# A decoder layer on one Trainium2 core: marks of all expert pairs counted at once in bf16, gates brought to their slots on chip

## Chip, cores and metric

One NeuronCore of a Trainium2 chip runs the whole layer in one launch. The time is device microseconds (us) of that core; lower is better. Values are f32 unless a tile is said to be bf16.

## What is computed

`x` (2048 tokens of 256) goes through causal self-attention on Plücker lines, cross-attention over 1601 context rows, and a mixture of 16 experts. The change lies in the last part:

```python
affinity = _sinkhorn(affinity_logits)          # 16 experts x 2048 tokens, 6 rounds
gates, idx = jax.lax.top_k(affinity, CAP)      # the 64 best tokens of each expert
expert_in = jnp.take_along_axis(x[:, None, :, :], idx[..., None], axis=2)
h = jax.nn.gelu(jnp.einsum('becd,edf->becf', expert_in, w1) + b1[None, :, None, :])
expert_out = jnp.einsum('becf,efd->becd', h, w2) + b2[None, :, None, :]
out = out.at[jnp.arange(b)[:, None, None], idx].add(gates[..., None] * expert_out)
```

## The kernel before

Everything up to the router is ordered by a planner; the change does not touch it. After it comes the tail, whose order on each engine is written by hand. It has three stages.

**Router.** VectorE does the Sinkhorn rounds, then finds the 64 best values of each of 8 chunks of tokens (`best_v`, `best_i`), and from them the limit of each expert (`limit`, L1590), counts over the chunks (`sums`), and the place at which each chunk's tokens go in its expert's list. It shifts each chunk's indices there in six doublings (L1619, L1620). TensorE turns and adds between these steps, and fills its waits with products that nobody reads: `keep_busy(n)` issues n of 128x256 (L1787). The engines run in order, so such products also hold back what stands behind them.

**Lists and pairs.** The product `tops` (L1957) adds the shifted lists up; VectorE casts them to `idx_gather` (L1629) and `idx_f`. Experts are taken in 8 pairs, 64 rows for each expert. GpSimd issues one indirect DMA for each pair's token rows (`gather_x`, L1090) and one for their affinities (L1098), from `affin_d`, which SyncE stored before. A token can be in both experts of a pair. So for each pair VectorE writes 128x256 of marks (`mark`, L1640 and L1641), TensorE adds them up over the partitions (`pair_sum`, L2008), and VectorE reads which rows repeat and which token numbers are free (`read_sums`, `place_rows`, L1648 to L1664). Two mark buffers are in turn.

**Experts.** For pair i: `expert_in(i)` turns the gathered rows (L1964), `hidden(i)` is the first product (L1977), `turn_hidden(i)` turns it (L1990), ScalarE does the gelu, `expert_out(i)` is the second product (L2001), `merge(i)` applies the gates and the merging of repeated rows (L2019), ScalarE copies the result (L1229), and GpSimd adds it to `out` by an indirect DMA (L1107), each behind the landing of the one before. SyncE loads the weights of experts 8 to 15 (L793, L798) and the bias rows (L966) as slots come free: the first of these wait for `hidden(0)` to be read on VectorE (`next_w1(0)`), and the others for later reads. Three PSUM banks (`g`) go round over the list `tail`: a step may write its bank only when VectorE has read the step three places before it.

## Time and profile before

| what | us |
|---|---|
| time of the runs shown, median (lowest, highest) | 1174.94 (1174.15, 1175.01) |
| profiled execution, its own time | 1175.17 |
| span of the profiled execution | 1173.4 |
| TensorE busy, VectorE busy, ScalarE busy, GpSimd busy in the span | 1105.5, 860.9, 718.2, 151.4 |

The span leaves out 1.8 us of the profiled execution's own time. Busy shares are averages over the whole program; the tail, from about 1030 us on, has other limits than the attention stages. The times in rows count from the start of the span.

### The profile page before, as it was taken

To read this page: it belongs to the slowest core of one execution; us is meant where nothing else is said; L and a number is where in the kernel's file an instruction comes from. 1 tells how busy PE (TensorE), PEld (TensorE's weight loads), DVE (VectorE), ACT (ScalarE), POOL (GpSimd) and SP (SyncE) were. 2 spreads that over 40 slices of the span, in tenths; PEclk is the share of its full clock that TensorE was granted. 3 is DMA by queue.
4 is the path that set the end of the run, shared out by engine and by line. 5 is a ranking of instruction groups with operands and counts; after the bars stand their busy time and mean duration, and the time that the engine had idled before them with its cause. 6 is when DMAs were issued, how large, how long until landed. Compare 5 with 4: busy or idle time off the path is not lost.

```text
span 1173.4 us, 30372 instructions
## 1 busy us (share of the span) xinstructions
PE 1105.5 (94%) x12600; PEld 525.7 (45%) x12600; DVE 860.9 (73%) x2017; ACT 718.2 (61%) x823; POOL 151.4 (13%) x260
## 2 busy tenths in 40 slices
PE   4788999999999999999999999999999999888997
PEld 2443433332432323544454456555555552467554
DVE  4888565487788878889788889788878980378631
ACT  0345567887678867677776877677785789310111
POOL 3024125112111011000001000010001000000522
PEclk9898999999999989999999999999999999998999
DMA  5113408722011000103232200111102000088696
GB/s 168 32 36 95 117 16 152 169 36 74 25 35 40 16 15 2 53 28 88 79 101 65 88 18 28 52 47 30 30 20 65 17 16 2 24 310 193 184 345 173
DMA packets 81562, 90.45 MB, mean 77 GB/s; under 512 B 18208, under 2 KB 73952, under 8 KB 81424
## 3 DMA queue, kind: packets, MB, share of 16 engines
q1 hardware_dynamic: 75264, 80.04, 23.9%
q10 hardware_dynamic: 4368, 6.29, 1.7%
q0 software_dynamic: 1792, 2.16, 1.0%
q8 instruction: 100, 1.64, 0.6%
q14 instruction: 38, 0.31, 0.1%
HBM read 73.42 MB, written 15.04 MB: 75 GB/s over the span
## 4 chain that ended last, share of the span: by engine, by line
PE 76%; DVE 11%; DMA 5%; issue 4%; ACT 2%; POOL 1%; ACTq 0%; DVEq 0%; POOLq 0%
PE po L1778 24%; PE g L1886 16%; PE scores L1754 15%; PE scores L1758 6%; PE g L1871 3%; PE g L1831 2%; ACT probs L1194 2%; DMA out<-self_region,idx_scatter 1%; DVE mx L1465 1%; PE g L1821 1%; PE g L1861 1%; DMA out<-wo_sb,idx_scatter 1%; PE scores L1787 1%; DMA out<-wxq_sb,idx_scatter 1%; PE g L1977 1%
## 5 line engine op out<-in xcount | busy, mean ns | idle before, releaser
L1194 ACT ACTIVATE probs<-scores 128x1024 f32<-128x1024 f32 (+2 forms) x736 | 677.0, 968 | 239.7 <-PE scores L1754 131.3
L1465 DVE TENSOR_REDUCE mx<-g 128x1 f32<-128x400 f32 (+1 forms) x1024 | 526.4, 567 | 86.2 <-PE g L1886 76.6
L1886 PE MATMUL g<-cross_region,even_region 96*32 96x400 bf16 (+1 forms) x4096 | 310.5, 338 | 0.4
L1754 PE MATMUL scores<-even_region,cross_region 99*32 99x512 bf16 (+1 forms) x3264 | 255.0, 379 | 2.5 <-ACT probs L1194 2.5
L1778 PE MATMUL po<-probs,cross_region 128*32 128x512 f32 (+1 forms) x1664 | 225.3, 594 | 0.8 <-ACT probs L1194 0.8
L1886 PEld LDWEIGHTS g<-cross_region,even_region 96*32 96x32 bf16 x4096 | 123.3, 95 | 182.9 <-DVE mx L1465 81.9
L1778 PE MATMUL po<-probs,self_region 128*32 128x512 f32 (+3 forms) x1280 | 152.1, 550 | 4.5 <-POOL probs L1055 3.9
L1754 PEld LDWEIGHTS scores<-even_region,cross_region 99*32 99x32 bf16 (+1 forms) x3264 | 100.9, 96 | 96.0 <-issue 42.6
L1758 PE MATMUL scores<-self_region 36*128 36x512 bf16 (+3 forms) x640 | 104.9, 360 | 7.2 <-ACT probs L1194 6.8
L1055 POOL TENSOR_SCALAR_AFFINE_SELECT probs<-probs 128x256 f32<-128x256 f32 x128 | 58.8, 468 | 276.7 <-ACT probs L1194 275.9
L1022 POOL TENSOR_TENSOR rstd<-mv,half 128x1 f32<-128x1 f32 x48 | 26.7, 556 | 518.5 <-DVE mv L1273 518.3
L1758 PEld LDWEIGHTS scores<-self_region 36*128 36x128 bf16 x640 | 26.6, 94 | 126.1 <-ACT probs L1194 76.9
L1778 PEld LDWEIGHTS po<-probs,cross_region 128*32 128x32 f32 (+1 forms) x1664 | 56.8, 110 | 24.9 <-ACT probs L1194 6.4
L1224 ACT ACTIVATE even_region<-scores 128x1024 f32<-128x1024 f32 x4 | 4.1, 1026 | 85.8 <-PE scores L1990 85.8
L1787 PE MATMUL scores<-xbo_sb,ident 128*128 128x256 f32 x190 | 51.4, 424 | 0.0
L1778 PEld LDWEIGHTS po<-probs,self_region 128*32 128x32 f32 x1280 | 30.9, 110 | 33.6 <-POOL probs L1055 13.5
L1821 PE MATMUL g<-ident,xn 128*128 128x128 f32 x96 | 21.0, 305 | 25.7 <-DVE xn L1327 25.6
L1787 PEld LDWEIGHTS scores<-xbo_sb,ident 128*128 128x128 f32 x190 | 39.5, 214 | 6.3 <-issue 0.2
L1439 DVE RECIPROCAL rsum<-g 128x16 f32<-128x16 f32 x32 | 8.2, 255 | 45.7 <-PE g L1861 45.5
L1831 PE MATMUL g<-wself_sb,xn_t 128*128 128x512 f32 x64 | 34.3, 662 | 0.1
L1450 DVE TENSOR_TENSOR xb<-g,xb 128x256 f32<-128x256 f32 x32 | 13.6, 424 | 28.1 <-PE g L1871 27.3
L1821 PEld LDWEIGHTS g<-ident,xn 128*128 128x128 f32 x96 | 10.4, 146 | 42.9 <-issue 31.0
(287 smaller groups left out, 881.3 us busy)
## 6 DMA issues: line engine op xcount, KB each, us to landing
cross_region<-in_w SPq DMA_DIRECT2D x16, 1024.0 KB, 12.8
even_region<-xq_d SPq DMA_DIRECT2D x192, 64.0 KB, 2.3
self_region<-in_w ACTq DMA_DIRECT2D x6, 1024.0 KB, 6.6
self_region<-in_w SPq DMA_DIRECT2D x6, 1024.0 KB, 13.8
cross_region<-xk_d SPq DMA_DIRECT2D x24, 200.1 KB, 8.0
xb<-in_x SPq DMA_DIRECT2D x32, 128.0 KB, 2.8
xb<-x_d SPq DMA_DIRECT2D x32, 128.0 KB, 2.4
probs<-in_w SPq DMA_DIRECT2D x4, 1024.0 KB, 13.2
```

The lines of the kernel that those rows point to most:

```text
L1022: pool.tensor_tensor(rstd[:, u % 4:u % 4 + 1], mv[:, u % 4, 1:2], half[:, 0:1], ALU.pow).then_inc(rstd_ready, 1)
L1055: pool.affine_select(out=d, in_=d, compare_op=ALU.is_ge, fill=0.0, base=0, pattern=[[0, 2], [1, P]], channel_multiplier=-1).then_inc(mask_ ...
L1194: act.activation(probs[0:rows, s % 4, :, off:], ps[s % 2][0:rows, :, off:], ACT.Exp, scale=LSCALE if QUADS[n][0] == "self" else 1.0).then_ ...
L1465: dve.reduce_max(mx[:, k % 2, b, h, c:c + 1], g[:, 0:n_keys], AX_X).then_inc(g_free, 1)
L1754: mm = pe.matmul(ps[s % 2][c:c + n_keys, a, :], k_cross[0:NS * DH + 3, h, i * P + c:i * P + c + n_keys], rhs, start=True, stop=True)
L1758: mm = pe.matmul(ps[s % 2][0:rows, a, off:], lhs, rhs, start=True, stop=True)
L1778: mm = pe.matmul(po[32 * a:32 * a + 32, off:], v[0:rows, i, h * VW:h * VW + 32], probs[0:rows, s % 4, a % 2, off:], start=(i == 0), stop=e ...
L1787: pe.matmul(ps[0][:, 0, 0:D], ident[:, :], xbo_sb[:, :], start=True, stop=True)
L1821: mm = pe.transpose(g[:, k * P:(k + 1) * P], xn[:, norm_no[u] % 2, k * P:(k + 1) * P], ident[:, :])
L1831: pe.matmul(g[:, :], xn_t[:, k, c + 1:c + 1 + P], wself_sb[:, k, 0:512], start=(k == 0), stop=False)
L1871: mm = pe.matmul(g[:, 0:D], attn_t[:, k, :], (wo_sb if step[1] == "self" else wxo_sb)[:, k, :], start=(k == 0), stop=(k == DK - 1))
L1886: mm = pe.matmul(g[q:q + 32, 0:n_keys], q_max[k % 2][0:NS * DH, h, b * P + q:b * P + q + 32], k_cross[0:NS * DH, 4 * (k % 4) + h, start:st ...
```

## The change

The marks of all eight pairs are written by one VectorE instruction of 128x1024 in bf16 (`mark_tokens`) and counted by two bf16 products, before the first gathered rows are turned. Which rows repeat is read from eight small products (128x64) of the lists themselves, which follow `tops`. The gates are no longer stored and gathered: VectorE shifts the values `best_v` as it shifted the indices, in `shifted_v`, and one more product (`gates`) adds them up to their slots. Of the unread products, 15 become 18 ahead of `best_t`, and 12 become 17 ahead of `tops`; two after `tops` become one and two, written to `po`. Lines that are only "..." stand for what is left out.

```diff
-    affin_d = nc.dram_tensor("affin_d", (T, E), F32, kind="Internal").ap()
...
-        kept = o_region[:, 1344:1344 + CAP]
+        kept = late_region[:, 264:264 + CAP]
...
-        bits = o_region[:, 1436:1442]
-        others = o_region[:, 1442:1448]
+        bits = late_region[:, 328:334]
+        others = late_region[:, 334:340]
...
-        picked_affin = late_region[:, 256:256 + E // 2 * E].rearrange("p (i e) -> p i e", e=E)
+        gates = late_region[:, 256:256 + E // 2]
+        shifted_v = [even_region[:, 1024 + 2 * CAP * r:1024 + 2 * CAP * (r + 1)] for r in range(2)]
...
-        marks = [attn[:, :], attn_t[:, :, :].rearrange("p k n -> p (k n)")]
+        marks = o_region[:, 1536:2048].bitcast(BF16).rearrange("p (i n) -> p i n", i=E // 2)
+        ones_b = attn[:, 0:P // 2].bitcast(BF16)
...
-        affin_stored = sem("affin_stored")
-        gates_gathered = [sem(f"gates_gathered{i}") for i in range(E // 2)]
+        values_ready = sem("values_ready")
...
         tail = ["col_turn", "col_back"] + [("col_sum", it) for it in range(SINK_ITERS)]
...
-                 ("h", 1, 0), ("h", 1, 1)]
+                 ("h", 1, 0), ("h", 1, 1), "gates"]
         for i in range(E // 2):
...
-            sp.wait_ge(router_pe, 3 + SINK_ITERS)
-            sp.dma_start(affin_d.rearrange("(b p) e -> p b e", p=P), affin[:, :, :]).then_inc(affin_stored, 16)
...
+            pool.wait_ge(g_full, NG)
+            pool.memset(attn[:, 0:P // 2], BF16_ONES).then_inc(const_ready, 1)
...
             pool.wait_ge(picked, 2)
-            pool.wait_ge(affin_stored, 16)
...
             for i in range(E // 2):
...
                     gather_x(i + 2)
-                pool.indirect_dma_start(
-                    picked_affin[:, i, :], None, affin_d, bass.IndirectOffsetOnAxis(idx_gather[:, i:i + 1], 0)
-                ).then_inc(gates_gathered[i], 16)
...
             for i in range(E // 2):
...
+            def move(bufs, k):
+                src, dst = bufs[k % 2], bufs[1 - k % 2]
+                link(dve.tensor_scalar(kept, src[:, CAP:2 * CAP], others[:, k:k + 1], None, ALU.mult))
+                return dve.scalar_tensor_tensor(out=dst[:, CAP:2 * CAP],
+                                                in0=src[:, CAP - (1 << k):2 * CAP - (1 << k)],
+                                                scalar=bits[:, k:k + 1], in1=kept, op0=ALU.mult, op1=ALU.add)
...
-                src, dst = shifted[k % 2], shifted[1 - k % 2]
-                link(dve.tensor_scalar(kept, src[:, CAP:2 * CAP], others[:, k:k + 1], None, ALU.mult))
-                last = dve.scalar_tensor_tensor(out=dst[:, CAP:2 * CAP], in0=src[:, CAP - (1 << k):2 * CAP - (1 << k)],
-                                                scalar=bits[:, k:k + 1], in1=kept, op0=ALU.mult, op1=ALU.add)
+                last = move(shifted, k)
...
-            def mark(i):
-                if i >= 2:
-                    dve.wait_ge(pair_sums, i - 1)
-                link(dve.tensor_scalar(marks[i % 2][:, 0:P], ident[:, :], idx_f[:, i:i + 1], None, ALU.mult))
-                dve.tensor_scalar(marks[i % 2][:, P:2 * P], row_no, idx_f[:, i:i + 1], None,
-                                  ALU.is_equal).then_inc(marked, 1)
-            def read_sums(q):
-                four = slice(4 * q, 4 * q + 4)
-                dve.wait_ge(pair_sums, 4 * q + 4)
-                sums = ps[q][:, :, :].rearrange("p a b -> p (a b)").rearrange("p (i n) -> p i n", i=4)
-                link(dve.tensor_tensor(mix[:, four, 0:CAP], sums[:, :, 0:CAP],
-                                       idx_f[:, four].unsqueeze(2).broadcast_to((P, 4, CAP)), ALU.is_equal))
-                dve.scalar_tensor_tensor(out=unused[:, four, :], in0=sums[:, :, P:2 * P], scalar=0.0,
-                                         in1=row_no.unsqueeze(1).broadcast_to((P, 4, P)), op0=ALU.is_equal,
+            def mark_tokens():
+                dve.tensor_tensor(marks, row_no.unsqueeze(1).broadcast_to((P, E // 2, P)),
+                                  idx_f.unsqueeze(2).broadcast_to((P, E // 2, P)), ALU.is_equal).then_inc(marked, 1)
+            def read_sums():
+                dve.wait_ge(pair_sums, 2)
+                link(dve.tensor_tensor(mix[:, :, 0:CAP], ps[0][:, 0, :].rearrange("p (i n) -> p i n", n=CAP),
+                                       idx_f.unsqueeze(2).broadcast_to((P, E // 2, CAP)), ALU.is_equal))
+                counts_of = ps[1][:, :, :].rearrange("p a b -> p (a b)").rearrange("p (i n) -> p i n", n=P)
+                dve.scalar_tensor_tensor(out=unused, in0=counts_of, scalar=0.0,
+                                         in1=row_no.unsqueeze(1).broadcast_to((P, E // 2, P)), op0=ALU.is_equal,
                                          op1=ALU.mult).then_inc(sums_read, 1)
...
             def place_rows():
-                dve.wait_ge(sums_read, 2)
+                dve.wait_ge(sums_read, 1)
...
-                dve.wait_ge(gates_gathered[i], 16)
-                for e in range(2):
-                    rows = slice(CAP * e, CAP * (e + 1))
-                    last = dve.tensor_scalar(mix[rows, i, :], mix[rows, i, :],
-                                             picked_affin[rows, i, 2 * i + e:2 * i + e + 1], None, ALU.mult)
-                last.then_inc(mixed, 1)
+                dve.tensor_scalar(mix[:, i, :], mix[:, i, :], gates[:, i:i + 1], None, ALU.mult).then_inc(mixed, 1)
...
-            for i in range(4):
-                mark(i)
+            mark_tokens()
+            for r in range(2):
+                link(dve.memset(shifted_v[r][:, 0:CAP], 0.0))
+            link(dve.scalar_tensor_tensor(out=shifted_v[0][:, CAP:2 * CAP], in0=row_no[:, 0:CAP], scalar=n_here,
+                                          in1=best_v, op0=ALU.is_lt, op1=ALU.mult))
+            link(move(shifted_v, 0))
+            link(move(shifted_v, 1))
             expert_in(0)
             expert_in(1)
-            mark(4)
-            mark(5)
-            read_sums(0)
+            link(move(shifted_v, 2))
+            read_sums()
             hidden(0)
-            mark(6)
-            mark(7)
             expert_in(2)
-            read_sums(1)
+            for k in range(3, 5):
+                link(move(shifted_v, k))
+            move(shifted_v, 5).then_inc(values_ready, 1)
             hidden(1)
+            g = tail_full(dve, "gates")
+            for e in range(2):
+                last = dve.tensor_copy(gates[CAP * e:CAP * (e + 1), :],
+                                       g[0:CAP, 0:E].rearrange("p (i e) -> p e i", e=2)[:, e, :])
+                if e == 0:
+                    link(last)
+            last.then_inc(g_free, 1)
+            dve.wait_ge(g_free, TF["gates"])
             place_rows()
             for i in range(E // 2):
...
-            def keep_busy(n):
+            def keep_busy(n, bank=ps[0][:, 0, 0:D]):
...
-                    pe.matmul(ps[0][:, 0, 0:D], ident[:, :], xbo_sb[:, :], start=True, stop=True)
+                    pe.matmul(bank, ident[:, :], xbo_sb[:, :], start=True, stop=True)
...
-            keep_busy(15)
+            keep_busy(18)
             g = tail_bank(pe, "best_t")
...
-            keep_busy(12)
+            keep_busy(17)
             g = tail_bank(pe, "tops")
...
             pe.matmul(g[0:CAP, 0:E], shifted[0][:, CAP:2 * CAP], same_expert[:, 0:E], start=True, stop=True).then_inc(g_full, 1)
+            pe.wait_ge(exp_done, 2 * len(QUADS))
+            for i in range(E // 2):
+                mm = pe.matmul(ps[0][:, 0, CAP * i:CAP * (i + 1)], same_expert[:, 2 * i:2 * i + 1].broadcast_to((P, P)),
+                               shifted[0][:, CAP:2 * CAP], start=True, stop=True)
+            mm.then_inc(pair_sums, 1)
...
-                    pe.wait_ge(sums_read, i + 1)
+                    pe.wait_ge(sums_read, 1)
...
-            def pair_sum(i):
-                pe.wait_ge(marked, i + 1)
-                pe.matmul(ps[i // 4][:, i % 4 // 2, i % 2 * 2 * P:(i % 2 + 1) * 2 * P], ones[:, :], marks[i % 2],
-                          start=True, stop=True).then_inc(pair_sums, 1)
+            def count_marks():
+                pe.wait_ge(const_ready, 17)
+                pe.wait_ge(marked, 1)
+                for half_of in range(2):
+                    mm = pe.matmul(ps[1][:, half_of, :], ones_b, marks[:, 4 * half_of:4 * half_of + 4, :],
+                                   start=True, stop=True)
+                mm.then_inc(pair_sums, 1)
...
-            keep_busy(2)
-            pe.wait_ge(exp_done, 2 * len(QUADS))
-            for i in range(4):
-                pair_sum(i)
+            pe.wait_ge(o_free, len(evacs))
+            keep_busy(1, po[:, 0:D])
+            count_marks()
+            keep_busy(2, po[:, 0:D])
             expert_in(0)
             expert_in(1)
             hidden(0)
-            pair_sum(4)
-            pair_sum(5)
             expert_in(2)
-            pair_sum(6)
-            pair_sum(7)
             hidden(1)
+            g = tail_bank(pe, "gates")
+            pe.wait_ge(values_ready, 1)
+            pe.matmul(g[0:CAP, 0:E], shifted_v[0][:, CAP:2 * CAP], same_expert[:, 0:E], start=True, stop=True).then_inc(g_full, 1)
             turn_hidden(0)
             for i in range(E // 2):
...
```

How the instructions move. TensorE from the product `tops` to the first hidden product: before, with the pair sums as L2008,

```order
L1787 MATMUL scores<-xbo_sb,ident 128x256 x12
L1957 MATMUL g<-bo_sb,o_region 64x16
L1787 MATMUL scores<-xbo_sb,ident 128x256 x2
L2008 MATMUL scores<-attn,late_region 128x256
L2008 MATMUL scores<-attn_t,late_region 128x256
L2008 MATMUL scores<-attn,late_region 128x256
L2008 MATMUL scores<-attn_t,late_region 128x256
L1964 MATMUL g<-ident,self_region 128x128 x4
L1977 MATMUL g<-self_region 64x512 x8
```

and in the changed kernel, where L1962 is `tops`, L1966 the list products, L2021 the count and L1988 the hidden product:

```order
L1792 MATMUL scores<-xbo_sb,ident 128x256 x17
L1962 MATMUL g<-bo_sb,o_region 64x16
L1966 MATMUL scores<-o_region,bo_sb 128x64 x8
L1792 MATMUL po<-xbo_sb,ident 128x256
L2021 MATMUL scores<-o_region,attn 128x512 x2
L1792 MATMUL po<-xbo_sb,ident 128x256 x2
L1975 MATMUL g<-ident,self_region 128x128 x4
L1988 MATMUL g<-self_region 64x512 x8
```

The four pair sums ahead of the first transposes are gone; eight list products, two counts and one more unread product stand there. TensorE between `hidden(0)` and `hidden(1)`, before:

```order
L2008 MATMUL scores<-attn,late_region 128x256
L2008 MATMUL scores<-attn_t,late_region 128x256
L1964 MATMUL g<-ident,wo_sb 128x128 x2
L2008 MATMUL scores<-attn,late_region 128x256
L2008 MATMUL scores<-attn_t,late_region 128x256
L1977 MATMUL g<-self_region 64x512
```

and in the changed kernel, with the end of `hidden(1)` and the product of the gates (L2046) behind it:

```order
L1975 MATMUL g<-ident,wo_sb 128x128 x2
L1988 MATMUL g<-self_region 64x512
...
L1988 MATMUL g<-cross_region,self_region 64x512
L2046 MATMUL g<-bo_sb,even_region 64x16
L2001 MATMUL scores<-ident,even_region 128x128 x8
```

Four pair sums have left this place and one small product has come behind `hidden(1)`. VectorE in the changed kernel, from the marks (L1639) to the reading of `hidden(0)` (L1674); L1610 and L1611 are one doubling of the values, L1665 the copies of turned rows, L1644 and L1647 the reading of the sums:

```order
L1639 TENSOR_TENSOR o_region<-bv_sb 128x1024
L1690 MEMSET even_region 128x64 x2
L1691 SCALAR_TENSOR_TENSOR even_region<-bv_sb,o_region 128x64
...
L1665 COPY self_region<-g 128x256 x2
L1610 TENSOR_SCALAR late_region<-even_region,late_region 128x64
L1611 SCALAR_TENSOR_TENSOR even_region<-even_region,late_region 128x64
L1644 TENSOR_TENSOR o_region<-scores,bv_sb 128x8x64
L1647 SCALAR_TENSOR_TENSOR o_region<-scores,bv_sb 128x1024
L1674 TENSOR_TENSOR even_region<-g,even_region 128x512 x2
```

Before, eight pairs of L1640 and L1641 and two readings of half the size stood between L1630 and `hidden(1)`.

## Rows read from the trace of the kernel before

**Rows 1.** Window: PE, PEld, DVE, ACT, POOL busy us, clock, DMA share, GB/s.

```profile
1110.00:1120.00 10.00, 10.00 (x75) 5.48 (x70) 2.70 (x6) 1.29 (x2) 1.62 (x1) 1.00 1.04 285
```

**Rows 2.** Chain that ended last: start us, us, what.

```profile
1114.71 9.84 DMA out<-self_region,idx_scatter
...
1158.15 3.79 DMA out<-wxq_sb,idx_scatter
...
1167.26 1.55 POOL out L1107
```

**Rows 3.** Timeline of ScalarE: the last copy.

```profile
1166.06 0.37 ACT L1229 COPY wxo_sb<-po 128x256 f32<-128x256 f32 x1 [4.48 <-PE po L2019]
```

**Rows 4.** Timeline of TensorE, limit stage; each f32 product counts as two matmuls.

```profile
1056.40 6.64 PE L1787 MATMUL scores<-xbo_sb,ident 128*128 128x256 f32 x30
1064.59 0.27 PE L1930 MATMUL g<-ident,o_region 128*64 128x128 f32 x1 [1.55 <-DVE o_region L1562]
...
1066.91 9.48 PE L1787 MATMUL scores<-xbo_sb,ident 128*128 128x256 f32 x30
1076.31 0.38 PE L1947 MATMUL g<-o_region,bo_sb 16*128 16x8 f32 x2
...
1078.45 5.43 PE L1787 MATMUL scores<-xbo_sb,ident 128*128 128x256 f32 x24
1086.42 0.37 PE L1957 MATMUL g<-bo_sb,o_region 128*64 128x16 f32 x2 [2.54 <-DVE o_region L1620]
```

**Rows 5.** Windows of 2 us: the clock after each of two waits.

```profile
1066.00:1068.00 2.00, 2.00 (x11) 1.62 (x12) 1.49 (x6) 0.00 (x0) 0.00 (x0) 0.50 1.02 229
1086.00:1088.00 2.00, 1.57 (x5) 1.39 (x6) 1.28 (x7) 0.00 (x0) 0.52 (x1) 0.53 0.00 0
```

**Rows 6.** Timeline of VectorE around the limit.

```profile
1075.16 0.42 DVE L1567 FIND_INDEX8 o_region<-o_region,even_region 128x8 uint32<-128x256 f32 x1
1076.80 0.17 DVE L1590 COPY o_region<-g 128x8 f32<-128x8 f32 x1 [1.22 <-PE g L1947]
```

**Rows 7.** Timeline of GpSimd, first gathers; landing time of the second.

```profile
1087.48 1.21 POOL L1090 DMA_INDIRECT self_region<-xn_d,idx_gather  x1 [52.58 <-DVE idx_gather L1629]
1089.00 0.96 POOL L1090 DMA_INDIRECT self_region<-xn_d,idx_gather  x1 [0.31 <-issue]
...
DMA to landing us min/median/max: 2.8/2.8/2.8
```

**Rows 8.** Timeline of TensorE, first transposes to the last second product.

```profile
1091.44 0.89 PE L1964 MATMUL g<-ident,self_region 128*128 128x128 f32 x4
1092.54 3.65 PE L1977 MATMUL g<-self_region 128*64 128x512 f32 x16 [0.21 <-DVE self_region L1668]
...
1098.71 0.64 PE L1977 MATMUL g<-self_region 128*64 128x512 f32 x1
...
1107.89 3.62 PE L2001 MATMUL g<-self_region,even_region 128*64 128x256 f32 x32
...
1161.10 0.43 PE L2001 MATMUL g<-cross_region,self_region 128*64 128x256 f32 x1
```

**Rows 9.** Timelines and chain: rows nearest to the new instructions.

```profile
1078.02 0.35 PE L1952 MATMUL g<-o_region,bo_sb 128*128 128x2 f32 x2 [0.26 <-DVE o_region L1594]
1078.23 0.36 PE L1953 MATMUL g<-o_region,bo_sb 128*128 128x2 f32 x2
...
1082.94 0.30 DVE o_region L1620
...
1103.73 1.22 DVE L1657 TENSOR_REDUCE bv_sb<-o_region 128x8 f32<-128x1024 f32 x1
```

**Rows 10.** Queue of SyncE: first and last of the late loads.

```profile
1096.95 0.50 SPq L966 DMA_DIRECT2D even_region<-in_b  x1
...
1147.27 3.40 SPq L798 DMA_DIRECT2D probs<-in_w  x1
...
probs<-in_w SPq DMA_DIRECT2D x1, 1024.0 KB, 12.6
```

## Prediction

> **What bounds the kernel now.** I read the chain that ended last from its end backwards. Its last part is the eight indirect DMAs that add the expert rows to `out`, from 1114.71 on. Each waits for the landing of the one before: 9.84 us for the first, 3.79 for the sixth, and the last is issued at 1167.26 [rows 2]. Read alone, this says that the additions are the bound. The timeline of ScalarE corrects it: the last copy, which the last addition needs, begins at 1166.06 and takes 0.37 [rows 3]. So it is done at 1166.43, 0.83 before the last issue. Two chains arrive together, the additions and TensorE's expert products, and TensorE has no free time in the expert stage (10.00 of 10 us busy, clock 1.00, DMA share 1.04 [rows 1]). An edit pays only if it starts both chains sooner, so the question is when `expert_out(0)` starts; before, that is 1107.89 [rows 8]. The end also depends on the late weight loads, which fill the DMA engines [rows 1].
>
> **Unread products.** The 15 ahead of `best_t` end at 1063.04 (1056.40 + 6.64), and `best_t` comes at 1064.59 after 1.55 us of idle time. The clock is then 0.50 in the window of 1066 to 1068 [rows 4, 5], its lower level of 1.2 GHz. The 15 products ahead of `limit` take 9.48 us where the first 15 took 6.64, 2.8 us more [rows 4]. VectorE has ended its own searches at 1075.58 and gets the limit only at 1076.80 [rows 6]. A product costs 0.443 us at the full clock (6.64 / 15), so 18 end at 1064.4, just ahead of 1064.59: they delay nothing and leave 0.2 us idle instead of 1.55. I take it that the clock then stays at 2.4 GHz. The products ahead of `limit` end near 1073.6, TensorE is no longer the later one, and VectorE goes on at 1075.6: **1.2 us**. Lower end nothing (the clock falls all the same); upper end 1.2, since VectorE's searches bound it.
>
> The 17 ahead of `tops`: 12 take 5.43 us, 0.453 each, so 17 take 7.7. From 1078.45 they end at 1086.15, against `tops` at 1086.42 [rows 4]. Both shift together, so they are hidden by VectorE's shifting, with 0.27 us to spare at the full clock. Without that cover each costs 0.45 or, at half the clock, 0.9.
>
> **From the lists to `hidden(0)`.** The gathers follow the lists as before. The second is issued at 1089.00, lands 2.8 later, at 1091.8 [rows 7], and `hidden(0)` begins at 1092.54 [rows 8]. In between stand both transposes and a copy, because the pair sums held the first transpose until the second gather had landed. In the changed kernel TensorE has, behind `tops`, eight list products, a count in two, and three unread products. The list products are nearest to L1952 and L1953, which start 0.21 apart [rows 9]: 8 x 0.21 = 1.7 us (upper end 3.5, the price of unread products, 8 x 0.443). The three unread products are 1.35, the counts at most as much as a 128x256 f32 product each, 0.9. In all 3.6 to 4.0 us behind `tops` (1086.42 + 0.37 = 1086.8), so 1090.4 to 1090.8: about when the first gather lands (1087.48 + 3.0), and ahead of the second. The first transpose and its copy are then over before 1091.8, and `hidden(0)` follows the second transpose by some 0.3: 1092.2, **0.35 us** sooner. Lower end: list products at 3.5 push this to 1092.6 or so, no gain; upper end 0.5.
>
> VectorE's marks: 128x1024 lies nearest to the reduce of 128x1024, 1.22 us [rows 9]; below it can't be under half of that. They are needed when the list products are over, 1.7 us after `tops`, and it has them about 0.3 us later than that, which the one unread product ahead of the count covers.
>
> **Between `hidden(0)` and `expert_out(0)`.** From 1096.19 (1092.54 + 3.65) to 1098.71 TensorE does four pair sums and one pair of transposes [rows 8]. Only the transposes stay, 0.22: **2.3 us**. Behind `hidden(1)` comes the product of the gates, **-0.2** [rows 9]. Could VectorE now be late? After the second copy it has one doubling of the values (0.6), the reading of both sums (0.7 and 1.2, by the row of 128x1024), then `hidden(0)`'s first half (0.7): 3.2 us behind a copy that ends 0.6 after `hidden(0)` begins. That is 3.8, where TensorE needs the bank back after 3.65 + 0.22. It is nearly a tie; I take off **0.1**, and the lower end is 1 us. Behind the reading of `hidden(1)` stand the gate copies and the eight instructions of `place_rows`, the longest of them 1.22 us [rows 9]; I put both together at 4.2, and the copy of `xe` 3 behind them at 0.4. They begin near 1099.5 in the changed kernel and end near 1104.1, and `expert_out(0)` wants the bank of `xe` 3 at 1104.3. That is a second near tie: nothing is taken off, and each 0.1 us by which VectorE is later there comes off the gain. The gathers and the copy of the affinities that go take GpSimd time which lies beside other work.
>
> Sum for TensorE: 1.2 + 0.35 + 2.3 - 0.2 - 0.1 = 3.55 us sooner at `expert_out(0)`. All later steps of TensorE, and the first addition, shift with it.
>
> **What comes late next.** The late loads start when `hidden(0)` is read (1096.95 [rows 10]). That trigger comes only 1.2 + 0.3 = 1.5 us sooner, because the saving of 2.3 lies behind it, and from there the DMA engines are full. Six token gathers no longer stretch into that time, perhaps 0.6 us of transfer, and the second trigger comes 3.6 sooner into engines that are not quite full: together the loads end 2 to 2.5 us sooner. Before, the last one is issued at 1147.27 and lands after 12.6, 1159.9 [rows 10]; `expert_out(7)` wants it at 1161.10 [rows 8], a slack of 1.2. Then it lands at 1157.6 and is wanted at 1157.55: the slack is gone. The additions meet the same: the sixth was quick, 3.79, since the loads were ending; issued 3.5 sooner it has 3 us of loads before it. I take off **0.7** for both (bounds 0 and 2.0, the case where the loads keep their time but for 1.5).
>
> 3.55 - 0.7 = 2.85. Against the profiled execution's own 1175.17 that is 1172.3. The median of the runs shown is 0.2 under that execution, which may be in the clock's part of the tail; so I say 1172.2.
>
> **A rule against the change.** The first gathers are issued while VectorE works on the marks and doublings; in the rows the first takes 1.21 on GpSimd and the second 0.96, with VectorE busy there too [rows 7]. The Trainium skill, SBUF — State Buffer, section on the doors (the "DVE blocks DMA" trap), says that a DMA issued by GpSimd can't get its descriptors written while VectorE runs an instruction that takes both ports. By the rows, the most that such a wait can have cost a gather is 0.25 us (1.21 - 0.96). This is a rival with 3 in 100: both first gathers later by 0.25 each, the time 1172.7. By that rule it would come through the memsets and multiplications, which are in both kernels.
>
> **Rivals.**
> Forecast as above, 50 in 100: 1171.3 to 1173.0.
> The clock falls ahead of `limit` all the same, 22 in 100. For it: the short products of `best_t` and the candidates keep TensorE half idle after the long ones, and 1.55 us of idle time sufficed before. The 1.2 us is lost: 1173.4.
> The late loads set the end, 18 in 100. For it: DMA share 1.04 [rows 1]. If only the first trigger's 1.5 us come through, 1175.17 - 1.5 = 1173.7.
> Slower, 7 in 100: the longer rows of unread products become the path. If the clock is at its lower level when the 17 begin and stays there, they take 17 x 0.886 = 15.1 us where VectorE's chain leaves 8.0 (1078.45 to 1086.42 [rows 4]). The other gains are 3.55 - 1.2 = 2.35, so the 17 make the kernel slower from a length of 10.3 us on; at full length they give 1175.2 + 7.1 - 2.35 = 1179.9.
> The additions alone being slowed by as much as they start sooner is the upper part of the third case, up to 1174.
>
> **How the numbers follow.** 0.2% of this time is 2.35 us, which is about what a measurement can tell; it lies at 1172.6, close to the forecast. Faster by more: most of the forecast's 50 and a little of the others, 52. Slower by more: most of the slow case and nothing else, 5. Within: 43. The range reaches over the two cases at 1173.4 and 1173.7 with their uncertainty of 0.3: 1170.9 to 1174.0. The lower end is the sum with no loss to the loads, 1175.17 - 3.55 = 1171.6, less the 0.2 of the median, and 0.5 for additions that find the engines freer.
>
> **What would show it.** Right: granted clock 1.00 in 1066 to 1076, the copy of the limit 1.2 us sooner; `hidden(0)` at about 1091.0, `hidden(1)` at 1094.9, `expert_out(0)` at 1104.3; the last load landing near 1157.6; the last addition issued near 1164.4. Wrong: clock 0.5 before `limit`; VectorE's L1647 ending after TensorE wants the bank; idle time of TensorE on a load ahead of `expert_out(7)`; additions that land later after their issue than before; unread products that end after their list is ready.

## The result and the profile after

The changed kernel takes 1168.05 us (median of 5 runs, 1167.61 to 1169.26), the kernel before 1174.39 (5 runs, 1172.11 to 1175.01). The ratio is 0.9953 with a 95% interval of [0.9939, 0.9966]: 4.0 to 7.2 us faster, where 2.2 were forecast (1174.39 - 1172.2). Measured again on two chips, it was 0.9951 (e5) and 0.9953 (e16). The time lies 2.9 us below the lower end of the range, 1170.9. The profiled execution has a span of 1166.3 us (before 1173.4).

**A place to start from.** The two profiled spans differ by 7.1 us, but not all of it is the edit. TensorE's first short transpose behind the 15 (now 18) unread products stands at 1064.59 before [rows 4] and at 1061.49 after, 3.1 us sooner, and ahead of it the edit only adds three products that fill a wait. The windows far ahead of the edit show where most of such differences come from; the columns are as in [rows 1]. First before:

```profile
420.00:430.00 10.00, 8.51 (x69) 2.26 (x68) 5.65 (x16) 6.37 (x8) 0.00 (x0) 0.70 0.16 42
430.00:440.00 10.00, 10.00 (x102) 2.78 (x98) 7.04 (x14) 6.72 (x8) 0.00 (x0) 0.79 0.00 0
```

and the same stretch of the changed kernel:

```profile
420.00:430.00 10.00, 8.51 (x108) 2.91 (x104) 7.88 (x21) 7.86 (x9) 0.32 (x1) 1.00 0.14 42
430.00:440.00 10.00, 10.00 (x122) 2.97 (x116) 8.05 (x16) 8.21 (x9) 0.00 (x0) 1.00 0.01 2
```

TensorE is busy for 8.51 us of the first window in both, but gets through 69 products in one and 108 in the other: the granted clock was 0.70 and 0.79 in one execution and 1.00 in the other. By ScalarE's timelines, where both kernels have the same instructions up to here, before is 1.35 us ahead at 409.32 (410.67 after) and 3.24 us behind at 438.89 (435.65 after), so the fall costs about 4.6 us. Of the 16 later profiles four have a clock of 0.61 to 0.71 in the first of these windows (e2, e3, e8, e11), with and without parts of the edit. So I count from that transpose to the end: 108.8 us before (1173.4 - 1064.59), 104.8 after (1166.3 - 1061.49), **4.0 us shorter**.

TensorE's timeline of the changed kernel from there, to be held against [rows 4] and [rows 8]:

```profile
1061.49 0.27 PE L1935 MATMUL g<-ident,o_region 128*64 128x128 f32 x1 [0.25 <-DVE o_region L1558]
1063.41 6.74 PE L1792 MATMUL scores<-xbo_sb,ident 128*128 128x256 f32 x30
1071.34 0.35 PE L1952 MATMUL g<-o_region,bo_sb 16*128 16x8 f32 x2 [1.19 <-DVE o_region L1582]
...
1073.37 0.35 PE L1957 MATMUL g<-o_region,bo_sb 128*128 128x2 f32 x2 [0.61 <-DVE o_region L1590]
...
1073.81 9.27 PE L1792 MATMUL scores<-xbo_sb,ident 128*128 128x256 f32 x34
1083.01 0.29 PE L1962 MATMUL g<-bo_sb,o_region 128*64 128x16 f32 x2
1083.23 2.00 PE L1966 MATMUL scores<-o_region,bo_sb 128*128 128x64 f32 x16
...
1088.72 3.65 PE L1988 MATMUL g<-self_region 128*64 128x512 f32 x16
...
1101.92 3.62 PE L2012 MATMUL g<-self_region,even_region 128*64 128x256 f32 x32
```

The wait ahead of `best_t` is 0.25 us instead of 1.55, and the 15 products ahead of `limit` take 6.74 instead of 9.48. TensorE now waits for VectorE at `limit` (1.19), not the other way round. Then, new: the 17 ahead of `tops` take 9.27 us, and the timeline of VectorE shows who pays:

```profile
1072.16 0.17 DVE L1586 COPY o_region<-g 128x8 f32<-128x8 f32 x1
...
1083.34 0.35 DVE L1630 CAST idx_gather<-g 64x8 uint32<-64x8 f32 x2 [1.69 <-PE g L1962]
...
1090.49 1.23 DVE L1647 SCALAR_TENSOR_TENSOR o_region<-scores,bv_sb 128x1024 f32<-128x1024 f32 x1
1091.63 1.48 DVE L1674 TENSOR_TENSOR even_region<-g,even_region 128x512 f32<-128x512 f32 x2
```

It waits 1.69 us for `tops`. The 2-us windows give the reason, a low clock behind the limit, which no profile of another kernel here has at this place:

```profile
1066.00:1068.00 2.00, 2.00 (x11) 1.77 (x10) 1.86 (x7) 0.00 (x0) 0.00 (x0) 1.00 1.02 234
1074.00:1076.00 2.00, 2.00 (x6) 1.62 (x6) 1.79 (x9) 0.00 (x0) 0.00 (x0) 0.55 0.04 8
1076.00:1078.00 2.00, 2.00 (x7) 1.59 (x7) 1.67 (x10) 0.00 (x0) 0.00 (x0) 0.60 0.00 0
```

So the 4.0 us come about as: transpose to limit copy 12.21 to 10.67 (1.54 gained), limit copy to `tops` 9.62 to 10.85 (1.23 lost), `tops` to `hidden(0)` 6.12 to 5.71 (0.41), `hidden(0)` to `expert_out(0)` 15.35 to 13.20 (2.15), from there to the last copy of ScalarE 58.17 in both. The rest, 1.13 us, is at the very end, and the prediction does not have it. ScalarE's last copy and GpSimd's additions:

```profile
1160.09 0.37 ACT L1225 COPY wxo_sb<-po 128x256 f32<-128x256 f32 x1 [4.47 <-PE po L2033]
```

```profile
1118.69 1.56 POOL L1103 DMA_INDIRECT out<-self_region,idx_scatter  x1 [8.33 <-DMA out<-self_region,idx_scatter]
...
1134.31 1.55 POOL L1103 DMA_INDIRECT out<-wo_sb,idx_scatter  x1 [6.21 <-ACT wo_sb L1225]
...
1160.73 1.55 POOL L1103 DMA_INDIRECT out<-wxo_sb,idx_scatter  x1 [3.16 <-ACT wxo_sb L1225]
```

Only the second and third addition still wait for the landing of the one before; from the fourth on each waits for ScalarE's copy. The last is issued 0.64 us behind the start of the last copy, before 1.20 [rows 2, 3]: 0.56 less in this pair of profiles. And the span ends 5.57 us behind that issue instead of 6.14 (1173.4 - 1167.26): 0.57 more. The late loads, on SyncE's queue:

```profile
1093.14 1.13 SPq L966 DMA_DIRECT2D even_region<-in_b  x2
...
1097.09 1.12 SPq L966 DMA_DIRECT2D even_region<-in_b  x2
...
1139.04 3.36 SPq L798 DMA_DIRECT2D probs<-in_w  x1
...
probs<-in_w SPq DMA_DIRECT2D x1, 1024.0 KB, 12.7
```

The last one is issued 8.2 us sooner than before (1147.27 [rows 10]), or 5.1 sooner when counted from the transpose. It lands near 1151.7 (1139.04 + 12.7), 3.5 us ahead of `expert_out(7)`, which begins at 1155.20 by the chain that ended last (in e5 and e16 it lands 2.2 and 2.3 us ahead):

```profile
1155.20 3.60 PE g L2012 x32
```

### The profile page after: what moved, and what is told of

Same layout as the page of the kernel before. It is cut to its first block, busy times and chain, and to the rows that moved or that the text cites. A ratio compares the mean times of both kernels' runs of the same rounds, so it can differ in the third digit from the quotient of the medians.

```text
span 1166.3 us, 30403 instructions
## 1 busy us (share of the span) xinstructions
PE 1101.0 (94%) x12622; PEld 525.5 (45%) x12622; DVE 859.5 (74%) x2009; ACT 718.2 (62%) x823; POOL 145.6 (12%) x253
## 4 chain that ended last, share of the span: by engine, by line
PE 82%; DVE 10%; issue 3%; ACT 2%; POOL 1%; DMA 1%; ACTq 0%; DVEq 0%
PE po L1783 24%; PE g L1891 16%; PE scores L1759 15%; PE scores L1763 6%; PE g L1876 3%; PE g L1836 3%; PE g L1988 2%; PE g L2012 2%; ACT probs L1190 2%; PE g L1826 1%; PE g L1866 1%; PE scores L1792 1%; DVE mx L1461 1%; PE g L1882 1%; PE g L1870 1%
## 5 line engine op out<-in xcount | busy, mean ns | idle before, releaser
L1763 PE MATMUL scores<-self_region 36*128 36x512 bf16 (+3 forms) x640 | 103.5, 356 | 7.5 <-ACT probs L1190 7.2
```

The costliest lines, as they stand in the source:

```text
L1763: mm = pe.matmul(ps[s % 2][0:rows, a, off:], lhs, rhs, start=True, stop=True)
```

## Experiments

The kernels e1 to e4 ran on one chip, e5 to e8, e9 to e12 and e13 to e16 each on another. The kernel before took 1181.7, 1172.95, 1172.24 and 1173.36 us there (medians of 17 to 35 runs).

**e1, the unread products alone, in the kernel before.**

```diff
-            keep_busy(15)        # ahead of best_t
+            keep_busy(18)
-            keep_busy(12)        # ahead of tops
+            keep_busy(17)
```

> The kernel before with only the numbers of unread products changed (15 to 18 ahead of best_t, 12 to 17 ahead of tops). Theory A (the 18 keep the clock at its full level ahead of limit): granted clock 1.00 between the candidates and limit, the copy of the limit 1.2 us sooner against the stage's start, and the whole kernel 1 to 1.5 us under the kernel before. Rival B (the large surplus over the forecast comes from the products too): 3 us or more under it. Rival C (the surplus comes from a fall of the clock at 424 us, which is no part of the edit): this kernel's own profile may or may not have that fall, and its time goes with it by about 4.6 us.

Measured 1181.8 us, ratio 0.9999 [0.9987, 1.0011]. The clock was 1.00 from 1064 to 1080 and the limit copy came 10.65 us behind the transpose, yet no gain shows on this chip; the interval leaves room for 1.5 us. `hidden(0)` to `expert_out(0)` took 27.1 us. The chain of e1 in that stretch:

```profile
1094.22 3.29 another core or an unknown queue
...
1098.69 7.31 another core or an unknown queue
```

TensorE's and ScalarE's timelines, same kernel:

```profile
1098.16 1.09 PE L1990 MATMUL scores<-ident,even_region 128*128 128x128 f32 x8
1107.43 1.97 PE L1990 MATMUL scores<-ident,self_region 128*128 128x128 f32 x8 [8.18 <-DVE self_region L1677]
```

```profile
1106.20 1.02 ACT L1224 ACTIVATE even_region<-scores 128x1024 f32<-128x1024 f32 x1 [69.04 <-remote]
```

ScalarE's gelu needs only TensorE's transposes, which end at 1099.25; it starts at 1106.20. VectorE stands still from 1098.7 to 1106.1 as well. What both wait for is no instruction in the trace.

**e2, the changed kernel with the old numbers.**

```diff
-            keep_busy(18)
+            keep_busy(15)
-            keep_busy(17)
+            keep_busy(12)
```

> The changed kernel with the old numbers of unread products (15 ahead of best_t, 12 ahead of tops). Theory A: 1.2 us over the changed kernel by the limit stage, and up to 1 us more where a clock at 1.2 GHz behind tops holds back the list products; 1.2 to 2.2 us in all, the tail being 71.5 us or so in place of 69.9 from the first router instruction. Rival B (the products do more than that): 3 us or more over it. Rival (they do nothing): the same as the changed kernel.

Measured 1171.68 us, ratio 0.9914 [0.9895, 0.9932]: 10 us faster than before on that chip. `hidden(0)` to `expert_out(0)` is 13.2 us; the long wait of e1 is not there. `hidden(0)` follows `tops` by 7.91 us, where the changed kernel has 5.67 to 5.71: e12 returns to this.

**e3, the changed kernel with the affinities stored and gathered as before.** No doublings of values, no gates product; the marks and the products are the changed kernel's.

```diff
+                pool.indirect_dma_start(picked_affin[:, i, :], None, affin_d,
+                    bass.IndirectOffsetOnAxis(idx_gather[:, i:i + 1], 0)).then_inc(gates_gathered[i], 16)
-            pe.matmul(g[0:CAP, 0:E], shifted_v[0][:, CAP:2 * CAP], same_expert[:, 0:E], ...)
```

> The changed kernel with the gates stored and gathered as before, so without the doublings of the values and the product of the gates. Theory: the gates' part is worth nothing or a little less than nothing on TensorE (one product of 0.1 to 0.2 us is gone from the path), so the time is within 0.4 us of the changed kernel. Rival: the eight gathers of affinities slow GpSimd's token gathers and the late loads, and their removal was worth 0.5 us or more, so this one is slower by that.

Measured 1179.34, ratio 0.9978 [0.9967, 0.9989], with the long wait (21.5 us from `hidden(0)` to `expert_out(0)`).

**e4, the kernel before with two unread products in the wait near 421 us.**

```diff
+                    if step[1] == 3:
+                        for _ in range(2):
+                            pe.matmul(g[:, 0:D], ident[:, :], xbo_sb[:, :], start=True, stop=True)
                     pe.wait_ge(shift_split, step[1] + 1)
```

> The kernel before with two unread products of 128x256 in the PSUM bank of the fourth shift_turn, where TensorE waits 0.7 and 0.8 us near 421 us. Theory C (in most runs of the kernel before, the clock falls there for some 10 us and costs 4.6 us, whatever stands in the tail): granted clock 1.00 from 420 to 440, and 3 to 4.6 us under the kernel before in the median. Rival D (the whole surplus lies in the tail): within 0.5 us of the kernel before.

Measured 1182.17, ratio 1.0000 [0.9988, 1.0011]. Its profile has no low clock there, but neither has that of e1, which lacks the two products. Filling this wait changes nothing that the times show, on a chip where the long wait (24.2 us from `hidden(0)` to `expert_out(0)` in e4) hides much.

These four gave a new theory: gathering the affinities, which the prediction priced at nothing, costs time. The next four tested it, on a chip where no profile shows the long wait.

**e5, the changed kernel again.**

> The changed kernel itself, on the chip of the next three runs. If the chip has the long wait between hidden(0) and expert_out(0) in kernels that gather the affinities (27.1 us in e1 where the first chip's profile of before had 15.35), the changed kernel has 13.2 there and ends 10 to 13 us below before, of which the unread products (18 and 17 for 15 and 12) give at most 2: e2 had 1171.7 with the old numbers. Rival (no such wait, the gain is what the prediction summed): 3 to 6 us below before.

Measured 1167.61, ratio 0.9951 [0.9935, 0.9968]. The rival held: no long wait on this chip. This profile has the clock at 1.00 from 1064 on, and from the transpose to the end it is 103.5 us, 5.3 shorter than before. Its `tops` is on time:

```profile
1074.28 7.58 PE L1792 MATMUL scores<-xbo_sb,ident 128*128 128x256 f32 x34
1082.25 0.26 PE L1962 MATMUL g<-bo_sb,o_region 128*64 128x16 f32 x2 [0.39 <-DVE o_region L1611]
1082.44 2.00 PE L1966 MATMUL scores<-o_region,bo_sb 128*128 128x64 f32 x16
...
1087.92 3.65 PE L1988 MATMUL g<-self_region 128*64 128x512 f32 x16
```

**e6, the kernel before without the store and the gathers of the affinities.** The rows are weighted with a constant, so the gates are left out.

```diff
-            sp.dma_start(affin_d.rearrange("(b p) e -> p b e", p=P), affin[:, :, :]).then_inc(affin_stored, 16)
-                pool.indirect_dma_start(picked_affin[:, i, :], None, affin_d, ...)
-                                             picked_affin[rows, i, 2 * i + e:2 * i + e + 1], None, ALU.mult)
+                                             first_half[rows, 0:1], None, ALU.mult)
```

> Before without the store and the eight gathers of the affinities; the rows are weighted with a constant, so the gates are left out. Marks, pair sums and unread products are those of before. Theory (the small gathers hold TensorE's signals back between hidden(0) and expert_out(0)): 6 to 9 us below before, hidden(0) to expert_out(0) 15 to 16 us. Rival (the pair sums between the products cost the time, the gathers lie beside other work, as the prediction had it): within 0.5 us of before.

Measured 1170.72, ratio 0.9987 [0.9977, 0.9996]: 1.5 us by the ratio, 2.2 by the medians, between the two expectations. `hidden(0)` to `expert_out(0)` is 15.32, as before. SyncE's queue, with the second trigger of the late loads at 1099.76 and the last load:

```profile
1099.76 1.12 SPq L966 DMA_DIRECT2D even_region<-in_b  x2
...
1108.64 9.01 SPq L798 DMA_DIRECT2D self_region<-in_w  x2
...
1139.69 3.20 SPq L798 DMA_DIRECT2D probs<-in_w  x1
```

Its transpose stands at 1062.49, so the last load is issued 77.20 us behind it. That is as soon as in the changed kernel (77.55 to 78.38), although the order is the old one.

**e7, the changed kernel with the store and eight gathers that nobody reads.** GpSimd waits for them ahead of its first addition.

```diff
+            sp.dma_start(affin_d.rearrange("(b p) e -> p b e", p=P), affin[:, :, :]).then_inc(affin_stored, 16)
                     gather_x(i + 2)
+                pool.indirect_dma_start(picked_affin[:, i, :], None, affin_d, ...).then_inc(gates_gathered[i], 16)
             pool.wait_ge(placed, 1)
+            for r in range(E // 2):
+                pool.wait_ge(gates_gathered[r], 16)
```

> The changed kernel with the store and the eight gathers of the affinities put back at their old places, into columns that nobody reads; only GpSimd waits for them, at the row additions. Theory (the small gathers hold TensorE's signals back): 6 to 9 us above the changed kernel, with a wait of VectorE for hidden(1) of more than 4 us. Rival (they lie beside other work): within 0.5 us of the changed kernel.

Measured 1171.14, ratio 0.9987 [0.9973, 1.0001], 3.5 us above e5 by the medians. VectorE has no long wait; the theory's mechanism is not there, but the cost is. GpSimd's timeline shows it:

```profile
1111.70 1.62 POOL L1116 DMA_INDIRECT out<-self_region,idx_scatter  x1 [8.01 <-DMA late_region<-affin_d,idx_gather]
...
1154.40 1.55 POOL L1116 DMA_INDIRECT out<-wxq_sb,idx_scatter  x1 [6.55 <-DMA out<-wxq_sb,idx_scatter]
```

The last gather, issued at 1102.75, had not landed before 1111, and the additions were late from there to the end. The waits of TensorE show a second cost, a late load that it stood still for:

```profile
PE g L2025 <- DMA probs<-in_w: 1.2, 1, 1.2
```

**e8, the kernel before with the affinity gathers behind all token gathers.**

```diff
                 if i + 2 < E // 2:
                     gather_x(i + 2)
+            for i in range(E // 2):
                 pool.indirect_dma_start(picked_affin[:, i, :], None, affin_d, ...)
```

> Before with the eight affinity gathers behind all eight token gathers instead of between them. Theory A (any of the sixteen gathers that is under way with the late loads holds the signals back): same as before within 1 us. Theory B (what matters is a token gather that comes late because an affinity gather stands ahead of it): 5 to 9 us below before. Rival (gathers are hidden): within 0.5 us of before, and no long wait in either.

Measured 1172.56, ratio 0.9998 [0.9987, 1.0008]. Their place in the order is worth nothing that the interval shows (1.5 us at most).

**e9, as e7, but GpSimd waits for the idle gathers only at the end.**

```diff
-            for r in range(E // 2):
-                pool.wait_ge(gates_gathered[r], 16)
...
             pool.wait_ge(scattered, 16 * (E // 2))
+            for i in range(E // 2):
+                pool.wait_ge(gates_gathered[i], 16)
```

> As e7, but GpSimd waits for the eight idle affinity gathers only behind the last row addition; in e7 it waited ahead of the first, which began 3.75 us later than in the changed kernel. Theory (in e7 that wait cost the time, the gathers only load the DMA engines a little): ratio to before 0.995 to 0.997, that is 0 to 2 us above the changed kernel, the first addition about 6.9 us behind expert_out(0). Rival (the gathers themselves delay the late loads or the additions): ratio 0.998 to 0.999, the additions still the last chain.

Measured 1168.77, ratio 0.9978 [0.9965, 0.9990]. The median fits the theory (its wait was e7's largest cost), the ratio lies between both. In its profile every stage is as in e5, and only the end differs: 6.27 us from the last issue, not 5.57. So this profile shows 0.7 of the 3 us between the ratios.

**e10, e3 on this chip.**

> The changed kernel with the affinities stored and gathered again and read by expert_out, as e3, on another chip. Without the long wait of e1 and e3 between hidden(0) and expert_out(0), that stretch is 13.0 us (13.2 less the gates product), and the time is 0 to 2 us above the changed kernel: ratio to before 0.995 to 0.997. Rival: the affinity gathers cost 3 to 4 us in this form too, 0.998 to 0.999.

Measured 1169.42, ratio 0.9985 [0.9970, 0.9999], with 13.13 us from `hidden(0)` to `expert_out(0)`. By the median it is in the theory's range, by the ratio in the rival's. From the transpose to the end its profile has 104.2 us, 0.7 more than e5.

**e11, e1 on this chip.**

> Before with 18 and 17 unread products, as e1, on another chip. Prediction's term: 1.2 us for the clock, 1.55 by the profiles since; as before's runs have the low clock ahead of limit in most but not all cases, 0.8 to 1.5 us below before, ratio 0.9987 to 0.9993. Rival: the 17 cost as much as the 18 give (the first profile of the changed kernel had tops 1.2 us late), ratio 0.9995 to 1.0005.

Measured 1171.25, ratio 0.9994 [0.9982, 1.0006], 1.0 us below before by the medians, with an interval that holds zero. The profile says more. TensorE's timeline:

```profile
1084.20 0.26 PE L1957 MATMUL g<-bo_sb,o_region 128*64 128x16 f32 x2 [0.40 <-DVE o_region L1620]
...
1089.57 0.41 PE L1964 MATMUL g<-ident,self_region 128*128 128x128 f32 x2 [0.61 <-DMA self_region<-xn_d,idx_gather]
1089.91 3.65 PE L1977 MATMUL g<-self_region 128*64 128x512 f32 x16
```

With 17 products the clock is 1.00 behind `tops`, the pair sums are over before the second gather has landed, and `hidden(0)` follows `tops` by 5.71 us: as in the changed kernel, with all four pair sums still in their old place. GpSimd's last addition and SyncE's queue in the same kernel:

```profile
1164.20 1.55 POOL L1107 DMA_INDIRECT out<-wxo_sb,idx_scatter  x1 [3.10 <-ACT wxo_sb L1229]
```

```profile
1109.51 11.33 SPq L798 DMA_DIRECT2D self_region<-in_w  x2
...
1144.31 3.42 SPq L798 DMA_DIRECT2D probs<-in_w  x1
```

**e12, the changed kernel with 12 instead of 17 products ahead of `tops`, 18 ahead of `best_t`.**

```diff
-            keep_busy(17)
+            keep_busy(12)
```

> The changed kernel with 12 unread products ahead of tops, 18 ahead of best_t as it has. If the 17 only fill a wait, within 0.5 us of the changed kernel (ratio 0.9948 to 0.9957), or above it where the clock falls behind tops; if they are late in a share of the runs, up to 1 us below it (ratio 0.9940 to 0.9948).

Measured 1170.54, ratio 0.9988 [0.9974, 1.0001]: 2.9 us above e5, which ran on another chip, by the medians, and 4.3 by the ratios. It is the case that the expectation names beside its numbers, the clock that falls behind `tops`. TensorE's timeline of e12, against e5's above, tells why:

```profile
1082.75 0.26 PE L1962 MATMUL g<-bo_sb,o_region 128*64 128x16 f32 x2 [2.56 <-DVE o_region L1611]
1082.94 3.34 PE L1966 MATMUL scores<-o_region,bo_sb 128*128 128x64 f32 x16
...
1089.60 0.88 PE L1975 MATMUL g<-ident,self_region 128*128 128x128 f32 x4
1091.02 3.65 PE L1988 MATMUL g<-self_region 128*64 128x512 f32 x16 [0.54 <-DVE self_region L1665]
```

and its windows (TensorE's busy time, clock, DMA):

```profile
1084.00:1086.00 2.00, 2.00 (x11) 0.50 0.17 41
```

The list comes at the same time, but behind 2.56 us of idle time the clock is at its lower level. List products, counts, unread products and transposes all take longer, and `hidden(0)` follows `tops` by 8.27 us instead of 5.67: 2.6 us.

**e13, as e9, with one semaphore for the eight idle gathers instead of eight.**

```diff
-                ).then_inc(gates_gathered[i], 16)
+                ).then_inc(gates_gathered, 16)
```

> As e9 (the changed kernel with eight idle affinity gathers, waited for at the end), but all eight count on one semaphore instead of one each. From the issue of the last addition to the end of the span e9 has 6.27 us, the changed kernel 5.57. If the seven further semaphores that are used cost that time: 5.6 to 5.7. If the gathers or their store cost it: 6.2 to 6.3.

Measured 1170.21, ratio 0.9977 [0.9968, 0.9986]. The end took 6.33 us (last addition issued at 1162.07, span 1168.4). So the number of semaphores is not the cause of the 0.6. TensorE also waited 0.7 for the last load here, which was issued at 1144.20:

```profile
PE g L2024 <- DMA probs<-in_w: 0.7, 1, 0.7
```

**e14, the changed kernel with more products around the limit**, as an attempt to end the low clock of the first profile.

```diff
-            keep_busy(15)        # ahead of limit
+            keep_busy(17)
-            keep_busy(2)         # ahead of sums
+            keep_busy(3)
```

> The changed kernel with 17 instead of 15 unread products ahead of limit and 3 instead of 2 ahead of sums: TensorE's idle 1.19 and 0.61 us there become 0.3 and 0.2. If the clock falls there in a share of the runs, as in the first profile of the changed kernel (0.5 from 1074.1, tops 1.2 us late): median 0.2 to 1.0 us below e16, and fewer times at the upper end. Rival (that fall is rare, or the products are late themselves): within 0.3 us of e16.

Measured 1168.59, ratio 0.9962 [0.9947, 0.9976], above e16's 1167.80 by 0.8. Neither profile has the low clock there, and from the transpose to the end both have 103.7 us. The attempt shows no gain; whether it would end that fall is not tested.

**e15, the changed kernel with 15 instead of 18 products ahead of `best_t`.**

```diff
-            keep_busy(18)
+            keep_busy(15)
```

> The changed kernel with 15 instead of 18 unread products ahead of best_t. By the prediction's term the low clock ahead of limit comes back where it falls: limit 1.55 us later in such runs, the median 0.5 to 1.6 us above e16. Rival (only the 17 matter): within 0.3 us of e16.

Measured 1168.87, ratio 0.9964 [0.9950, 0.9979], 1.1 us above e16 by the medians. That is not shown to be the clock's doing: the intervals overlap, and e15's profile, whose own time of 1168.92 is its median, has no low clock ahead of the limit (10.66 us from the transpose to the limit copy, 103.9 to the end, against 103.7 in e16).

**e16, the changed kernel a third time.**

> The changed kernel again, as the measure for e13, e14 and e15 on their chip: ratio to before 0.9945 to 0.996; router to limit 43.8 us, limit to tops 9.62, tops to hidden(0) 5.7, hidden(0) to expert_out(0) 13.2, 5.57 from the last addition's issue to the end. On a chip with the long wait of e1 in before: ratio 0.989 to 0.991.

Measured 1167.80, ratio 0.9953 [0.9938, 0.9969].

## Why the prediction was wrong, by its steps

The direction was right, and two of the three gains on TensorE came for the reason given. The size was short by 2.4 us: 2.85 forecast; from the transpose on 5.3 in e5 and 5.1 in e16, against the profile of before.

**Clock ahead of the limit, forecast 1.2: right, larger.** 1.54 in the first profile. The upper end of 1.2 took VectorE's searches as the bound, but they are filled in between the rounds and shift with it: the limit copy comes right behind a search, without a wait. It is a gain of some executions only. With 15 products the transpose to the limit copy takes 12.21 us in the profiles of before and e8, 11.03 in e4 (clock 0.50 in 1062 to 1064) and 10.66 in e2, e6 and e15; with 18 it takes 10.65 to 10.67 in all twelve profiles. The rival in which the clock falls ahead of the limit all the same did not come. By the medians the 18 (e15) and the 18 and 17 together (e11) give about 1 us, which the intervals don't separate from nothing.

**The 17 ahead of `tops`, priced at nothing: wrong.** I looked only at what they cost and cited the cover that hides them. The time from `tops` to `hidden(0)` in the profiles shows what they give:

| from `tops` to `hidden(0)`, us | 12 products | 17 products |
|---|---|---|
| old order (pair sums first) | 6.12 (before), 6.11 (e8), 6.42 (e6), 7.15 (e4) | 5.67 (e1), 5.71 (e11) |
| new order (list products first) | 7.91 (e2), 8.27 (e12) | 5.66 to 5.72 (all) |

With 17 the two orders take the same. With 12 the clock falls behind `tops` in all six profiles, and that costs 0.4 to 1.5 us in the old order and 2.2 to 2.6 in the new one, where eight list products stand there at once. In the other direction, the first profile of the changed kernel has the clock at 0.55 while the 17 run, and `tops` 1.23 us late. That is the slower rival's mechanism at a small size. One of the three profiles of the changed kernel has it (e5 and e16 do not). How often it comes in the timed runs is not known.

**`hidden(0)` 0.35 sooner: the number was right (0.41; 0.45 in e5), the reason was not.** The prediction gave it to the pair sums, which held the first transpose until the second gather had landed. They did so because they ran at the low clock: in e1 and e11 they are still there and the gain is there too. So the 17 products give this gain, which the prediction had priced at nothing; that the two sizes agree is luck. The new order alone would have been a loss here (7.91 and 8.27 against 6.11 to 7.15).

**Pair sums 2.3, less gates 0.2, less VectorE 0.1: right** (2.0 forecast, 2.15 measured; 15.35 to 13.20, and 15.32 to 15.47 in e6, e8 and e11, which keep the pair sums). L1647 takes 1.23 us and ends at 1091.72. VectorE then does both halves of `hidden(0)` back to back and TensorE never waits for the bank. The gates product and the second near tie cost nothing more: `place_rows` and the copy of `xe` 3 end at 1101.43, 0.5 ahead of `expert_out(0)`.

**Late loads and additions, -0.7: this is the step that failed.** I let the loads end only 2 to 2.5 us sooner, so that the slack of the last one, 1.2, would be gone, and took 0.7 off with zero as the best case. The last load was issued 82.68 us behind the transpose before, and 77.55, 78.38 and 78.27 behind it in the three profiles of the changed kernel: 4.3 to 5.1 us sooner. Its slack grew from 1.2 to 3.5, 2.2 and 2.3 us, TensorE waits for none of the loads, and from `expert_out(0)` to the last copy it is 58.17 us in both. Nothing was lost, so the whole 0.7 was too much.

Why the loads came so much sooner has two candidates. One is the second trigger: before, it lay behind the pair sums, 6.2 us behind the first (1103.13 against 1096.95); after, it follows by 3.95 us (1097.09 against 1093.14). It is not enough: in e6 it follows by 6.15, as in the old order, and the last load comes 77.20 us behind the transpose all the same. What e6 lacks is the gathers of the affinities. In the old order with them the last load comes 82.68 (before), 80.70 (e8) and 80.41 (e11) behind the transpose, and the two L798 loads take 11.33 us to issue in e11 against 9.01 in e6. In the new order with them it is 78.37 (e9), 79.47 (e10), 80.83 (e7) and 81.37 (e13). These are single profiles and they scatter (e9 is as early as e5). They point to the gathers, and they speak against the second trigger as the only cause.

The additions lose nothing either. The 0.56 us that the last one gains is a gain against one profile: there it waited for a landing, but in e6, e8 and e11, of the old order too, the last five additions wait for ScalarE's copies and the last is issued 0.64 to 0.65 behind the copy's start. The two chains that the prediction saw arrive together, with the additions later by 0.83, were that execution's.

**Gathers of the affinities, "GpSimd time which lies beside other work": wrong.** They lie beside other work as long as one looks at GpSimd alone. As transfers they cost. Three kernels only add them back without a use (e7, e9, e13: 0.9987, 0.9978, 0.9977 against 0.9951 and 0.9953): 2 to 4 us by ratios and medians, 3.7, 0.7 and 1.9 us by their profiles from the transpose on. The intervals of e9 and e13 touch those of the changed kernel; e7's does not. e6, which takes them from the kernel before, gives 1.5 to 2.2. Three parts are seen. The end of the span lies 6.1 to 6.3 us behind the issue of the last addition in all ten kernels with these gathers and 5.6 to 5.7 in all eight without, while that addition lands 3.7 to 3.8 us after its issue in both. The last load is issued later in most, as above, and TensorE waits for it in e7 and e13, which is the rival of the late loads, in a kernel where I did not look for it. And on one chip there is the long wait.

**The sum, with the sizes measured (e5's profile against that of before):** 1.54 for the clock, 0.45 to `hidden(0)`, 2.14 to `expert_out(0)`, 0.01 to the last copy, 0.55 for the additions, 0.58 behind the last issue: 5.27 us. Against the 2.85 forecast that is 0.34, 0.10 and 0.14 more in the first three terms, the 0.7 that was taken off, and 0.55 and 0.58 that the prediction did not have: 2.4 in all. The medians on that chip differ by 5.3, but that match proves little. The profile of before is a slow execution of it (1175.17, above all five timed runs), with the low clock ahead of the limit and the late last addition; against e8's profile the same count gives 4.8 us, against e11's, which has the 18 and 17 products, 3.0. And the medians also hold what lies ahead of the transpose. Of before's 29 runs on e5's chip, the 15 with a mean granted clock of 0.976 to 0.979 average 1173.8 us and the other 14 average 1171.1, while all six runs of e5 are at 0.982 or more. How much of that is the fall near 424 us, which is not the edit's, and how much the clock ahead of the limit, the runs don't tell.

**What stays open.** First, the long wait between `hidden(0)` and `expert_out(0)`, in e1, e3 and e4, one chip. There e2 has no affinity gathers and no long wait, and e3 has both; the two differ by the gates and by the numbers of products, and e4, with the old numbers, has the wait. So it went with the gathers on that chip. But e7 to e11 and e13 have the gathers too, on three other chips, and no such wait. The kernel before, which has the gathers, took 1181.7 us on that chip. What the engines wait for the trace does not say, and the cause is not settled. Second, whether the store of the affinities or the gathers cost the 0.6 us at the end. Third, what decides in which execution the clock falls near 424 us, ahead of the limit or behind it, and how often it does in the timed runs. Fourth, which part of the loads' gain is the gathers' and which the second trigger's.

**The rule against the change.** In e5 the first gather takes 1.21 us and the second 0.96 while VectorE is at the marks (1.23 us, from 1083.32), two memsets (from 1084.50) and a doubling. It is what they took before [rows 7], where multiplications ran beside them but, other than the prediction says, no memsets.

```profile
1083.20 1.21 POOL L1089 DMA_INDIRECT self_region<-xn_d,idx_gather  x1 [50.82 <-DVE idx_gather L1630]
1084.71 0.96 POOL L1089 DMA_INDIRECT self_region<-xn_d,idx_gather  x1 [0.30 <-issue]
```

By the Trainium skill, SBUF — State Buffer, section "SBUF: two separate sides" (the "DVE blocks DMA" trap), they could have been held up. The trace does not agree: neither took longer than before.

## What to carry to other kernels

A filler that is priced by "it ends before its successor is wanted" is only half priced: ask what the clock will be for the work that stands right behind it, above all when an edit moves real work there. When an edit changes the filler and the order together, run all four combinations before a gain is given to one of them: here the number fitted and the reason did not. A small transfer that nobody waits for still takes its place among those that somebody waits for; price it where the DMA engines are full, by a kernel that has it without a use. Give a term that can be a gain an upper bound of its own. And read a gap of 0.5 us in more than one profile before it becomes a bound: the late last addition was in one execution of before and in no other kernel of its order.

## What the runs showed of the hardware

The same program's executions differ in when the granted clock falls. The same two waits of TensorE near 421 us, under 1 us each, were followed by 0.70 in the window in some profiles and by 1.00 in others, and the times of before spread over 7.1 us on one chip (1168.28 to 1175.36, 35 runs). Differences of single profiles have to be taken from a common instruction on, as here.

Chips differ too: before took 1181.7 us on one and 1172.2 to 1174.4 in the other sets of runs. On that one alone the three profiles of kernels with the affinity gathers have a long wait: VectorE, ScalarE and TensorE stand still together for 6.8 us in e1 (1099.25 to 1106.09) and 5.1 in e3 (1099.58 to 1104.69), and in e4 VectorE has three waits of 2.33, 3.09 and 3.17 us. In e1 the DMA share falls meanwhile from 1.04 (1100 to 1102) to 0.09 (1104 to 1106); in e3 it stays at 0.88 to 1.03 (1100 to 1106).
